# Four-head attention on one core: weighing rounds in two runs of three, maxima one slot sooner, three small VectorE operations on GpSimd

## The chip, the cores and the metric

The kernel runs on one core of a Trainium2 chip. The metric is the device time of one execution in microseconds (us). The core has a matmul engine (TensorE, in the rows PE, its weight loads PEld), three engines for elementwise work (VectorE or DVE, ScalarE or ACT, GpSimd or POOL) and SyncE, which issues transfers. Each engine runs its own list of instructions in order; semaphores tie the lists together. Matmul results land in PSUM, which has eight banks of 512 columns.

## What is computed

Two layers over 2048 rows of width 128; each layer is `x + s * silu(g)`, with an attention `s` and a feed-forward block `g`. The change lies in the attention inside `g` of the second layer: four heads of 32 columns, every row against all 2048 rows, with keys and values shared by the heads.

```
nx = _rmsnorm(X, g1)
Q = (nx @ Wq.T).reshape(B, S, H, dk).transpose(0, 2, 1, 3)
Kc = nx @ Wkc.T
Vc = nx @ Wvc.T
scores = jnp.einsum('bhsd,btd->bhst', Q, Kc) * scale
attn = jax.nn.softmax(scores, axis=-1)
out = jnp.einsum('bhst,btd->bhsd', attn, Vc)
out = out.transpose(0, 2, 1, 3).reshape(B, S, d) @ Wo.T
```

After it come a residual, a second norm, a router over eight experts and the experts themselves.

## The kernel before, in words

The 2048 query rows are cut into 16 tiles of 128. `shared_tile` of each engine is its work for one tile i; `over_tiles` calls it for 0 to 15. A tile has 16 slots t, one for each chunk of 128 keys.

In each slot TensorE makes one score matmul (L2050: keys of chunk t against the queries of all four heads, 512 columns) for tile i, and one maximum matmul (L2040: one head's queries against 512 keys) for a tile to come. ScalarE turns each score bank into exponentials in SBUF (L1543), VectorE reduces each maximum bank to one column (L1092). Scores rotate over three banks (2, 3, 4), maxima over three others (0, 1, 5): each engine can be at most three banks behind TensorE. A tile needs 16 maxima (`MU`); the first comes at slot `MAX_START` two tiles ahead, the last before the same slot one tile ahead.

The exponent needs the negated row maximum. Matmuls here take numbers rounded to a shorter format (fp32r), so the maximum, like the queries, is split into a high part and a low part, the rest. `cut_maximum` on VectorE makes the total (L1099), the high part (L1101) and the low part (L1103). `turn_maxima` (slot `TURN_SLOT` = 11) then transposes queries and maximum on TensorE (L2026, 98 rows), and ScalarE copies them (L1531); tile i+1's scores need that copy. Before, `turn_queries` (slot 6, L2017, 96 rows) transposed the queries of tile i+2 for the maxima, and ScalarE copied them (L1527) ahead of the exponentials of slot 6 and on. The queries' low part is a subtraction of VectorE in `query_tile` (L1131).

Weighing is the product of exponentials and values. Its 16 chunks are cut into six `ROUNDS`, five of three chunks and one of one. Three matmuls of a round work side by side on 32 columns each (L2060), and a fourth beside them (L2067) adds up the denominators. Its input is a sum of exponentials over chunks, made in `PIECES`: piece 0 is chunks 0 and 1, piece 1 is 2 to 4, piece 2 is 5 to 7, piece 3 is 8 to 10, piece 4 is 11 to 13. GpSimd makes these in `whole_sum`: a first addition (L773) and, for three chunks, a second (L778). The last piece (14, 15) is VectorE's (`last_sum`, L1109). The sums rotate over three buffers (`SUM_RING`): piece p waits for the round three before it. `ROUND_SLOT` says at the end of which slot a round stands in TensorE's list; 19 is slot 3 of the next tile. Before, this makes three runs of two rounds per tile: at slot 8, at slot 14 and at slot 3 of the next.

After the last round ScalarE copies the result (L1551), TensorE transposes it at slot 14 (`turn_rows`, L2074), VectorE takes the reciprocal of the denominators and adds the three parts (`shared_out`, L1119 and L1120), and a tile later divides (`shared_divided`, L1125). `PREP` puts preparations of the next stage into the list, one for each tile from 1 on: four projections or transposes at slot 2 or slot 9.

What follows is the code of this stage as far as the change reaches.

Of the kernel before, what the change touches and what calls it, by code (L numbers as in the profile page):

```python
# [6 lines left out]
P = 128  # L7
T = 2048
NT = T // P
D = 128  # L10
F32 = mybir.dt.float32
F32R = mybir.dt.float32r
# [3 lines left out]
ALU = mybir.AluOpType  # L16
# [25 lines left out]
HM = 4  # L42
DM = D // HM
SCM = float(DM) ** -0.5
R_ROWS = 3 * DM
# [6 lines left out]
NR = len(ROUNDS)  # L52
POOL_PIECES = NR - 1
SUM_RING = 3
ROUND_SLOT = (8, 8, 14, 14, 19, 19)
MU = HM * T // 512
MAX_BANKS = (0, 1, 5)
SCORE_BANKS = (2, 3, 4)
# [7 lines left out]
LAST_PREP = {(0, 2): ("omT", 3), (0, 4): ("mo", 3), (1, 1): ("nxT", 3), (1, 3): ("lg", 3)}  # L66
MAX_START = 9
QUERY_SLOT = 6
TURN_SLOT = 11
ROWS_SLOT = 14  # L70
OUT_SLOT = 14
SPLIT_SLOT = 3
OSTEPS = 2
SUM_PAIR = 2

E1 = 8
# [50 lines left out]
def at(a, i):  # L127

    if isinstance(i, int):
        return a[:, i]  # L130
    one = a[:, bass.ds(i, 1)]
    names = " ".join("abcd"[:len(one.shape) - 2])
    return one.rearrange(f"p o {names} -> p (o {names.split()[0]}) {' '.join(names.split()[1:])}")
# [8 lines left out]
def still(i, ahead):  # L142

    return not isinstance(i, int) or i + ahead < NT
# [34 lines left out]
def bass_recurrent_two_layers(nc, A, out):  # L179
# [4 lines left out]
    with ExitStack() as ctx:  # L184
# [117 lines left out]
        qkv = region.take(NT, D + 2 * DM)  # L302
        ka = region.take(NT, M_ROWS)
        crossT = region.take(T)
        qtile2 = region.take(2, HM, M_ROWS)
# [3 lines left out]
        om = region.take(NT, D)  # L309
        sp = region.take(SUM_RING, HM * P)  # L310
        mxp = region.take(HM, MU // HM)
        negm = region.take(HM)
        oT = region.take(HM * P)
        ol = region.take(HM, DM)
        rsm = region.take(HM)
# [75 lines left out]
        om_read = sem("om_read"); om_ready = sem("om_ready"); m_step = sem("m_step")  # L391
# [164 lines left out]
        def _(pool):  # L556
# [208 lines left out]
            def whole_sum(i, p, first):  # L765

                tiles = PIECES[p]
                o = sp[:, p % SUM_RING, :]
                held = lambda t: pm[:, t // 2 % HELD, t % 2 * HM * P:(t % 2 + 1) * HM * P]
                if not (first and p < SUM_RING):  # L770
                    pool.wait_ge(round_done, i * NR + p - SUM_RING + 1)
                pool.wait_ge(p_whole, i * NT + tiles[1] + 1)
                ins = pool.tensor_tensor(o, held(tiles[0]), held(tiles[1]), ALU.add)  # L773
                if len(tiles) == 3:
                    ins.then_inc(sum_step, 1)
                    pool.wait_ge(sum_step, i * (POOL_PIECES - 1) + p)
                    pool.wait_ge(p_whole, i * NT + tiles[2] + 1)
                    ins = pool.tensor_tensor(o, o, held(tiles[2]), ALU.add)  # L778
                ins.then_inc(sum_ready, 1)
# [3 lines left out]
            def low_rows(g):  # L783
                pool.wait_ge(xh_ready, g + 1)
                pool.tensor_tensor(xl[g], xnT[:, tokens(g)], xh[g].bitcast(F32), ALU.subtract).then_inc(xl_ready, 1)

            def shared_tile(i, parity, first=False, more=True):
                for p in range(POOL_PIECES):
                    whole_sum(i, p, first)
                if 0 <= i - HALVES_TILE < ES:  # L790
                    expert_halves(i - HALVES_TILE)
                if i in (6, 10, 14):
                    inverse_root(4, (i - 6) // 4, 1e-6)
                if i == 7:
                    low_rows(0)
# [35 lines left out]
        def _(dve):  # L831
# [251 lines left out]
                dve.wait_ge(rden_ready, (i + 1) // 2)  # L1083
                dve.tensor_tensor(o1T[:, (i - 1) * P:(i + 1) * P], parts[:, 0, :], rden[:, :], ALU.mult).then_inc(n_ready, 1)

            MSTEPS = 3

            def maximum(i, u):

                dve.wait_ge(mx_filled, i * MU + u + 1)  # L1090
                b = FIRST_BANKS[u % 5] if i == 0 else MAX_BANKS[(i * MU + u) % 3]
                dve.tensor_reduce(mxp[:, u // HM, u % HM:u % HM + 1], bank(b), AX.X, ALU.max).then_inc(mx_read, 1)  # L1092

            def cut_maximum(i, parity):

                high, low = (qtile2[:, parity, :, R_ROWS + n] for n in range(2))
                dve.wait_ge(mx_read, i * MU + MU)
                dve.wait_ge(tile_ready, i + 1)
                dve.tensor_reduce(negm[:, :], mxp[:, :, :], AX.X, ALU.max, negate=True).then_inc(m_step, 1)  # L1099
                dve.wait_ge(m_step, i * MSTEPS + 1)  # L1100
                dve.tensor_copy(high.bitcast(F32R), negm[:, :]).then_inc(m_step, 1)  # L1101
                dve.wait_ge(m_step, i * MSTEPS + 2)
                dve.tensor_tensor(low.bitcast(F32R), negm[:, :], high, ALU.subtract).then_inc(m_step, 1)  # L1103

            def last_sum(i):

# [15 lines left out]
            def shared_divided(i):  # L1122
                dve.wait_ge(om_read, OSTEPS * i + 2)
                dst = at(om, i).rearrange("p (h d) -> p h d", h=HM)
                dve.tensor_tensor(dst, ol[:, :, :], rsm[:, :].unsqueeze(2).broadcast_to([P, HM, DM]), ALU.mult).then_inc(om_ready, 1)  # L1125

            def query_tile(i, parity):

                q = at(qkv, i)[:, 0:D].rearrange("p (h d) -> p h d", h=HM)
                dve.wait_ge(q_high_ready, i + 1)  # L1130
                dve.tensor_tensor(qtile2[:, parity, :, 2 * DM:3 * DM].bitcast(F32R), q, qtile2[:, parity, :, 0:DM],  # L1131
                                  ALU.subtract).then_inc(q_low_ready, 1)
# [4 lines left out]
            for stage, i in chunk_order[:-1]:  # L1137
                if stage in steps:
                    steps[stage](i)
            cut_maximum(0, 0)  # L1140
            chunk_out(NT - 1)

            def residual1(g):
# [62 lines left out]
            def shared_tile(i, parity, first=False, more=True):  # L1206
                for t in range(NT):
                    for n, u in maxima_at(i, t):
                        if still(n, 0):
                            maximum(n, u)  # L1210
                            if u == MU - 1:
                                cut_maximum(n, 1 - parity)
                    if t == SPLIT_SLOT and still(i, 2):
                        query_tile(i + 2, parity)
                    if t == SPLIT_SLOT and i >= 2:
                        shared_divided(i - 2)
                    if t == 1 and not first:
                        last_sum(i - 1)
                    if t == 3 and i in (8, 12):
                        logits1((i - 8) // 4)  # L1220
                    if t == 4 and i in (6, 10, 14):
                        residual1((i - 6) // 4)
                    if t == 9 and i in (6, 10, 14):
                        row_stats((i - 6) // 4)
                        row_spread((i - 6) // 4)
                    if t == 9 and i == NT - 2:
                        router_differences(early_rows)
                    if t == 9 and i == NT - 1:
                        shares(early_rows, rexp_ready, 1)
                        largest(oh1, first_w, early_rows)  # L1230
                        first_place(oh1, early_rows)
                        without_first(early_rows)
                    if t == 10 and i == NT - 1:
                        logits1(2)
                        largest(oh2, second_w, early_rows)
                        first_place(oh2, early_rows)
                    if t == 12 and i == NT - 1:
                        weight_difference(early_rows)
                        router_differences(each_group[2])
                    if t == OUT_SLOT and not first:  # L1240
                        shared_out(i - 1)
# [1003 lines left out]
```

## Time and profile before

| What | Value |
|---|---|
| Median of three runs | 645.61 us (644.17 to 647.99) |
| Span of the profiled execution | 642.5 us |
| TensorE busy in it | 594.6 us, 93% |
| VectorE busy | 485.3 us, 76% |
| ScalarE busy | 351.0 us, 55% |
| GpSimd busy | 358.2 us, 56% |
| Stage of the change | 286.2 to 548.7 us |

The profile is of one execution; its span runs from the first instruction to the last, and the median of the runs is 3.1 us above it. Busy time is the sum over an engine's instructions. A wait is put down to the engine whose semaphore came last. Matmuls overlap with their successors, so the distance between two starts tells more than one duration.

### The profile page before, as it was taken

The numbers are of one execution on the slowest core, as the hardware profiler recorded it, in microseconds if no ns is written. First come the engines' busy times: TensorE is split into PE (matmuls) and PEld (weight loads), VectorE is DVE, ScalarE is ACT, GpSimd is POOL, SyncE is SP. The second block draws the span as 40 slices with busy tenths as digits, with TensorE's granted clock in tenths as the row PEclk, the third lists the DMA queues.
The fourth block names the chain that finished last, engine by engine and source line by source line (L and its number), as shares of the span: only waits on it lengthen the run. The fifth ranks groups of instructions, "written<-read, shape, count | busy, mean of one in ns | idle before, by whom it ended". The sixth has DMA issues, their size and how long they took to land.

```text
span 642.5 us, 12628 instructions
## 1 busy us (share of the span) xinstructions
PE 594.6 (93%) x4528; PEld 400.6 (62%) x4529; DVE 485.3 (76%) x1140; ACT 351.0 (55%) x710; POOL 358.2 (56%) x377
## 2 busy tenths in 40 slices
PE   4888899899989899969999999999999999999996
PEld 2566799667755566545555554555455543788885
DVE  5767345349968778898777787878887875798986
ACT  2645555336855456625777775767576665442222
POOL 6607400176647443607777778887787778415220
PEclk9999999999999999989999999999999998999998
DMA  9801122120000000000000000000000000000101
GB/s 294 347 2 50 51 66 65 41 55 6 0 2 2 2 3 3 3 1 1 1 1 1 1 2 1 2 0 2 1 2 1 1 2 1 1 2 1 34 0 34
DMA packets 16616, 17.33 MB, mean 27 GB/s; under 512 B 1712, under 2 KB 15024, under 8 KB 16176
## 3 DMA queue, kind: packets, MB, share of 16 engines
q1 hardware_dynamic: 15536, 14.49, 6.7%
q0 software_dynamic: 1024, 2.10, 1.1%
q8 instruction: 35, 0.57, 0.4%
q14 instruction: 21, 0.17, 0.1%
HBM read 11.34 MB, written 5.24 MB: 26 GB/s over the span
## 4 chain that ended last, share of the span: by engine, by line
PE 73%; DVE 12%; POOL 6%; issue 3%; ACT 3%; DMA 2%; SPq 0%; DVEq 0%; ACTq 0%; POOLq 0%
PE ps L2060 13%; PE ps L2050 10%; PE ps L2040 8%; PE ps L2188 5%; PE ps L1863 3%; DVE region L1092 3%; PE ps L1770 3%; PE ps L1753 3%; PE ps L2178 2%; PE ps L2180 2%; PE ps L2179 2%; POOL slots_in L626 2%; PE ps L1853 2%; PE ps L1951 2%; PE ps L1967 1%
## 5 line engine op out<-in xcount | busy, mean ns | idle before, releaser
L1092 DVE TENSOR_REDUCE region<-ps 128x1 f32<-128x512 f32 x256 | 160.7, 682 | 38.6 <-PE ps L2040 38.1
L1543 ACT ACTIVATE region<-ps 128x512 f32<-128x512 f32 x256 | 138.2, 600 | 58.7 <-PE ps L2050 58.7
L773 POOL TENSOR_TENSOR region<-region 128x512 f32<-128x512 f32 x80 | 108.9, 1364 | 42.2 <-ACT region L1543 38.5
L2050 PE MATMUL ps<-qmr,kr 98*128 98x512 f32 x256 | 111.9, 441 | 1.8 <-ACT region L1543 1.0
L2040 PE MATMUL ps<-kr,qmr 96*128 96x512 f32 x256 | 102.7, 411 | 2.2 <-DVE region L1092 1.5
L2060 PE MATMUL ps<-region 128*32 128x512 f32 x512 | 93.3, 609 | 0.0
L2067 PE MATMUL ps<-region,ones 128*32 128x512 f32 x192 | 93.1, 607 | 0.2 <-DVE region L1109 0.2
L778 POOL TENSOR_TENSOR region<-region 128x512 f32<-128x512 f32 x64 | 82.0, 1281 | 12.3 <-ACT region L1543 8.6
L2050 PEld LDWEIGHTS ps<-qmr,kr 98*128 98x128 f32 x256 | 48.8, 192 | 54.0 <-issue 28.8
L2040 PEld LDWEIGHTS ps<-kr,qmr 96*128 96x128 f32 x256 | 49.2, 193 | 15.5 <-DVE region L1092 9.0
L1647 ACT ACTIVATE region<-ps 128x512 f32<-128x512 f32 x36 | 21.6, 599 | 56.8 <-PE ps L2180 56.8
L664 POOL DMA_INDIRECT region<-slots_out,slot x16 | 15.2, 948 | 54.3 <-DMA slots_out<-og 49.7
L2060 PEld LDWEIGHTS ps<-region 128*32 128x32 f32 x512 | 18.8, 109 | 41.2 <-issue 27.7
L1265 DVE SCALAR_TENSOR_TENSOR xn<-ps,region,xn 128x128 f32<-128x128 f32 x144 | 40.5, 344 | 5.2 <-PE ps L2188 3.0
L1770 PE MATMUL ps<-region 128*128 128x128 f32 x272 | 37.0, 281 | 6.0 <-ACT region L1390 6.0
L1770 PEld LDWEIGHTS ps<-region 128*128 128x128 f32 x272 | 33.1, 191 | 11.7 <-ACT region L1390 11.2
L2188 PEld LDWEIGHTS ps<-e,region 128*128 128x128 f32 x288 | 36.9, 191 | 4.7 <-DVE region L1254 2.3
L2188 PE MATMUL ps<-e,region 128*128 128x128 f32 x288 | 38.5, 277 | 1.2 <-DVE region L1254 1.1
L1753 PE MATMUL ps<-region 128*128 128x512 f32 (+3 forms) x80 | 33.6, 554 | 3.9 <-ACT region L1378 2.5
L1390 ACT ACTIVATE region<-ps 128x512 f32<-128x512 f32 (+3 forms) x40 | 20.0, 531 | 22.8 <-PE ps L1762 22.5
L1378 ACT ACTIVATE region<-ps,nmax 128x1024 f32<-128x1024 f32 (+7 forms) x24 | 20.7, 865 | 19.6 <-DVE nmax L937 13.9
L933 DVE TENSOR_REDUCE rmax<-ps 128x1 f32<-128x512 f32 (+3 forms) x36 | 22.2, 623 | 11.5 <-PE ps L1753 11.0
(283 smaller groups left out, 1196.6 us busy)
## 6 DMA issues: line engine op xcount, KB each, us to landing
region<-in_w SPq DMA_DIRECT2D x2, 2048.0 KB, 12.8
slots_in<-zeros SPq DMA_DIRECT2D x1, 1536.0 KB, 9.0
region<-slots_in SPq DMA_DIRECT2D x6, 256.0 KB, 2.8
slots_out<-og SPq DMA_DIRECT2D x6, 256.0 KB, 2.4
e<-in_e SPq DMA_DIRECT2D x1, 1152.0 KB, 15.4
x<-in_x SPq DMA_DIRECT2D x4, 256.0 KB, 3.6
out<-y SPq DMA_DIRECT2D x3, 256.0 KB, 2.3
e<-in_e SPq DMA_DIRECT2D x1, 576.0 KB, 17.5
```

The source lines that it names most:

```text
L773: ins = pool.tensor_tensor(o, held(tiles[0]), held(tiles[1]), ALU.add)
L778: ins = pool.tensor_tensor(o, o, held(tiles[2]), ALU.add)
L1092: dve.tensor_reduce(mxp[:, u // HM, u % HM:u % HM + 1], bank(b), AX.X, ALU.max).then_inc(mx_read, 1)
L1265: dve.scalar_tensor_tensor(out=a_, in0=bank(4 + n_ % 2)[:, t * P:(t + 1) * P], scalar=c_, in1=a_, op0=ALU.mult, op1=ALU.add).then_inc(e_re ...
L1543: act.activation(pm[:, t // 2, t % 2 * HM * P:(t % 2 + 1) * HM * P], bank(SCORE_BANKS[n % 3]), ACT.Exp, scale=SCM).then_inc(p_whole, 1)
L1753: pe.matmul(scores_of(i)[:, c:c + m], qT[:, P * i:P * (i + 1)], kT[:, c:c + m], start=True, stop=True).then_inc(score_done, 1)
L1770: ins = pe.matmul(o[:, 0:D], probT[:, k % 2, P * (j - b):P * (j - b + 1)], v[:, j, :], start=(j == 0), stop=(j == i))
L2040: pe.matmul(bank(FIRST_BANKS[u % 5] if first else MAX_BANKS[(i * MU + u) % 3]), qm[0:R_ROWS, parity, h * P:(h + 1) * P], kr[0:R_ROWS, c:c ...
L2050: pe.matmul(bank(SCORE_BANKS[n % 3]), kr[0:M_ROWS, t * P:(t + 1) * P], qr[0:M_ROWS, parity, :], start=True, stop=True).then_inc(st_filled, 1)
L2060: pe.matmul(bank(6)[DM * g:DM * (g + 1), :], qkv[:, t, D + DM:D + 2 * DM], pm[:, t // 2 % HELD, t % 2 * HM * P:(t % 2 + 1) * HM * P], star ...
L2067: pe.matmul(bank(6)[DM * PARTS:P, :], ones[:, 0:DM], sp[:, r % SUM_RING, :], start=(r == 0), stop=(r == NR - 1), skip_group_check=True).th ...
L2188: ins = pe.matmul(bank(4 + n_ % 2)[:, t * P:(t + 1) * P], h1T[:, n_ % 2, t * P:(t + 1) * P], e2[:, e, :], start=True, stop=True)
```

## The change

`ROUND_SLOT` and `MAX_START` change, so weighing stands in two runs of three rounds (at slot 11 and at slot 3 of the next tile), and each maximum comes one slot sooner. The query subtraction, the division and the low part of the maximum go to GpSimd's list: the first two at the start of a tile, ahead of piece 0, the low part after piece 2. The very first low part, before tile 0, stays on VectorE, as do the last two divisions.

```diff
-ROUND_SLOT = (8, 8, 14, 14, 19, 19)
+ROUND_SLOT = (11, 11, 11, 19, 19, 19)
...
-MAX_START = 9
+MAX_START = 8
...
+MSTEPS = 3
+LOW_PIECE = 2
...
+            def query_low(i, parity):
+
+                q = at(qkv, i)[:, 0:D].rearrange("p (h d) -> p h d", h=HM)
+                pool.wait_ge(q_high_ready, i + 1)
+                pool.tensor_tensor(qtile2[:, parity, :, 2 * DM:3 * DM].bitcast(F32R), q, qtile2[:, parity, :, 0:DM],
+                                   ALU.subtract).then_inc(q_low_ready, 1)
+
+            def shared_divided(i):
+                pool.wait_ge(om_read, OSTEPS * i + 2)
+                dst = at(om, i).rearrange("p (h d) -> p h d", h=HM)
+                pool.tensor_tensor(dst, ol[:, :, :], rsm[:, :].unsqueeze(2).broadcast_to([P, HM, DM]), ALU.mult).then_inc(om_ready, 1)
+
+            def low_maximum(i, parity):
+
+                high, low = (qtile2[:, parity, :, R_ROWS + n] for n in range(2))
+                pool.wait_ge(m_step, i * MSTEPS + 2)
+                pool.tensor_tensor(low.bitcast(F32R), negm[:, :], high, ALU.subtract).then_inc(m_step, 1)
+
             def shared_tile(i, parity, first=False, more=True):
+                if still(i, 2):
+                    query_low(i + 2, parity)
+                if i >= 2:
+                    shared_divided(i - 2)
                 for p in range(POOL_PIECES):
                     whole_sum(i, p, first)
+                    if p == LOW_PIECE and more:
+                        low_maximum(i + 1, 1 - parity)
...
-            def cut_maximum(i, parity):
-
-                high, low = (qtile2[:, parity, :, R_ROWS + n] for n in range(2))
+            def high_maximum(i, parity):
+
                 dve.wait_ge(mx_read, i * MU + MU)
                 dve.wait_ge(tile_ready, i + 1)
+                if i > 0:
+                    dve.wait_ge(m_step, i * MSTEPS)
                 dve.tensor_reduce(negm[:, :], mxp[:, :, :], AX.X, ALU.max, negate=True).then_inc(m_step, 1)
                 dve.wait_ge(m_step, i * MSTEPS + 1)
-                dve.tensor_copy(high.bitcast(F32R), negm[:, :]).then_inc(m_step, 1)
-                dve.wait_ge(m_step, i * MSTEPS + 2)
-                dve.tensor_tensor(low.bitcast(F32R), negm[:, :], high, ALU.subtract).then_inc(m_step, 1)
+                dve.tensor_copy(qtile2[:, parity, :, R_ROWS].bitcast(F32R), negm[:, :]).then_inc(m_step, 1)
...
-                    if t == SPLIT_SLOT and still(i, 2):
-                        query_tile(i + 2, parity)
-                    if t == SPLIT_SLOT and i >= 2:
-                        shared_divided(i - 2)
```

What TensorE has in a row ahead of the turn of the maxima (L2026), in the kernel before; this is an ordinary tile, from the weighing at slot 8 on. L2060 and L2067 weigh, L2050 is a score, L2040 a maximum.

```order
L2060 MATMUL ps<-region 32x512 [waits p_whole] x3
L2067 MATMUL ps<-region,ones 32x512 [waits sum_ready]
L2050 MATMUL ps<-qmr,kr 128x512 [waits p_whole]
L2040 MATMUL ps<-kr,qmr 128x512 [waits mx_read,qm_ready]
L2050 MATMUL ps<-qmr,kr 128x512 [waits p_whole]
L2040 MATMUL ps<-kr,qmr 128x512 [waits mx_read]
L2050 MATMUL ps<-qmr,kr 128x512 [waits p_whole]
L2040 MATMUL ps<-kr,qmr 128x512 [waits mx_read]
L2026 MATMUL ps<-ident,region 98x128 [waits qm_ready,m_step]
```

The same place in the changed kernel: the last pair of the run, the turn (now L2047) and the weighing (L2081, L2088) behind it.

```order
L2071 MATMUL ps<-qmr,kr 128x512 [waits p_whole]
L2061 MATMUL ps<-kr,qmr 128x512 [waits mx_read]
L2047 MATMUL ps<-ident,region 98x128 [waits qm_ready,m_step]
L2047 MATMUL ps<-ident,region 98x128 x3
L2081 MATMUL ps<-region 32x512 [waits p_whole,oT_ready]
L2081 MATMUL ps<-region 32x512 [waits p_whole] x2
L2088 MATMUL ps<-region,ones 32x512 [waits sum_ready]
```

The weighing that stood three pairs ahead of the turn now stands behind it, and has a third round.

GpSimd's list over one tile before: one addition for piece 0, then pairs of additions for pieces 1 to 4, then one expert's subtraction.

```order
L773 TENSOR_TENSOR region<-region 128x512 [waits p_whole,round_done] x2
L778 TENSOR_TENSOR region<-region 128x512 [waits p_whole,sum_step]
L773 TENSOR_TENSOR region<-region 128x512 [waits p_whole,round_done]
L778 TENSOR_TENSOR region<-region 128x512 [waits p_whole,sum_step]
L726 TENSOR_TENSOR ehl<-e13,ehl 128x256 [waits eh_ready]
```

And in the changed kernel, where additions are L775 and L780: from the second addition of piece 1 on, to the first work of the next tile.

```order
L780 TENSOR_TENSOR region<-region 128x512 [waits p_whole,sum_step]
L775 TENSOR_TENSOR region<-region 128x512 [waits p_whole,round_done]
L780 TENSOR_TENSOR region<-region 128x512 [waits p_whole,sum_step]
L805 TENSOR_TENSOR region<-region 128x4 [waits m_step]
L775 TENSOR_TENSOR region<-region 128x512 [waits p_whole,round_done]
L780 TENSOR_TENSOR region<-region 128x512 [waits p_whole,sum_step]
L775 TENSOR_TENSOR region<-region 128x512 [waits p_whole,round_done]
L780 TENSOR_TENSOR region<-region 128x512 [waits p_whole,sum_step]
L728 TENSOR_TENSOR ehl<-e13,ehl 128x256 [waits eh_ready]
L793 TENSOR_TENSOR region<-region 128x4x32 [waits q_high_ready]
L799 TENSOR_TENSOR region<-region 128x128 [waits om_read]
```

L805 is the low part of the maximum, which `m_step` of the turn waits for; L793 is the query subtraction, L799 the division.

## Rows read from the trace of the kernel before

**Rows 1.** Chain that ended last: start us, length us, engine, line.

```profile
317.84 0.56 PE ps L2060 x3
...
333.71 0.56 PE ps L2060 x3
...
381.18 0.56 PE ps L2060 x3
...
398.63 0.56 PE ps L2060 x3
```

**Rows 2.** Busy time of each engine (instructions), clock, DMA in the stage.

```profile
286.20:548.70 262.50, 257.79 (x1480) 141.19 (x1480) 210.96 (x415) 175.13 (x363) 206.44 (x169) 0.98 0.00 1
```

**Rows 3.** Timeline of TensorE, tile 3: start us, length us, then the instruction.

```profile
338.94 0.63 PE L2060 MATMUL ps<-region 128*32 128x512 f32 x3
...
340.79 0.50 PE L2050 MATMUL ps<-qmr,kr 98*128 98x512 f32 x1
...
341.36 0.40 PE L2050 MATMUL ps<-qmr,kr 98*128 98x512 f32 x1
...
341.83 0.40 PE L2050 MATMUL ps<-qmr,kr 98*128 98x512 f32 x1
...
342.31 0.60 PE L2017 MATMUL ps<-ident,region 128*96 128x128 f32 x4
...
343.76 0.63 PE L2060 MATMUL ps<-region 128*32 128x512 f32 x3
...
345.62 0.50 PE L2050 MATMUL ps<-qmr,kr 98*128 98x512 f32 x1
...
347.13 0.60 PE L2026 MATMUL ps<-ident,region 128*98 128x128 f32 x4
...
348.98 0.60 PE L2074 MATMUL ps<-ident,region 128*128 128x128 f32 x4
```

**Rows 4.** Timeline of ScalarE, tile 3.

```profile
342.95 0.59 ACT L1527 ACTIVATE qmr<-ps 96x512 fp32r<-96x512 f32 x1 [0.47 <-PE ps L2017]
343.44 1.55 ACT L1543 ACTIVATE region<-ps 128x512 f32<-128x512 f32 x3
```

**Rows 5.** Timeline of GpSimd, tile 3; in brackets its idle time and releaser.

```profile
340.12 1.38 POOL L773 TENSOR_TENSOR region<-region 128x512 f32<-128x512 f32 x1 [0.21 <-PE ps L2067]
...
344.17 1.28 POOL L773 TENSOR_TENSOR region<-region 128x512 f32<-128x512 f32 x1 [0.75 <-ACT region L1543]
345.52 1.30 POOL L778 TENSOR_TENSOR region<-region 128x512 f32<-128x512 f32 x1
```

**Rows 6.** Timeline of VectorE, tile 3.

```profile
339.88 0.28 DVE L1131 TENSOR_TENSOR region<-region 128x128 fp32r<-128x128 f32 x1
...
341.56 3.14 DVE L1092 TENSOR_REDUCE region<-ps 128x1 f32<-128x512 f32 x5 [1.20 <-PE ps L2040]
344.73 0.17 DVE L1099 TENSOR_REDUCE region<-region 128x4 f32<-128x16 f32 x1
344.94 0.54 DVE L1101 CAST region<-region 128x4 fp32r<-128x4 f32 x1
...
350.13 0.53 DVE L1120 TENSOR_REDUCE region<-ps 128x128 f32<-128x384 f32 x1
```

**Rows 7.** Groups of GpSimd's instructions by form: count, busy us, mean ns.

```profile
L713 POOL TENSOR_TENSOR region<-region 128x128 fp32r<-128x128 f32 x4 | 1.8, 439 | 0.0
...
L598 POOL TENSOR_TENSOR msq<-msq,mv 128x4 f32<-128x4 f32 x4 | 0.8, 202 | 0.3
```

**Rows 8.** Tile 15: two stretches as in rows 2, then TensorE's timeline.

```profile
532.30:534.30 2.00, 1.53 (x5) 0.56 (x3) 1.34 (x2) 2.00 (x7) 1.69 (x2) 1.00 0.01 4
...
536.60:539.90 3.30, 3.30 (x17) 0.63 (x10) 0.00 (x0) 1.27 (x3) 2.67 (x3) 0.50 0.00 0
...
536.97 1.09 PE L2060 MATMUL ps<-region 128*32 128x512 f32 x3
...
537.82 1.09 PE L2060 MATMUL ps<-region 128*32 128x512 f32 x3
```

More of the change, by code:

```diff
@@ L1084, in chunk_out @@
                 dve.tensor_tensor(o1T[:, (i - 1) * P:(i + 1) * P], parts[:, 0, :], rden[:, :], ALU.mult).then_inc(n_ready, 1)
-            MSTEPS = 3
             def maximum(i, u):
@@ L1139, in _ @@
                     steps[stage](i)
-            cut_maximum(0, 0)
+            high_maximum(0, 0)
+            dve.wait_ge(m_step, 2)
+            dve.tensor_tensor(qtile2[:, 0, :, R_ROWS + 1].bitcast(F32R), negm[:, :], qtile2[:, 0, :, R_ROWS], ALU.subtract).then_inc(m_step, 1)
             chunk_out(NT - 1)
@@ L1211, in shared_tile @@
                             if u == MU - 1:
-                                cut_maximum(n, 1 - parity)
-                    if t == SPLIT_SLOT and still(i, 2):
-                        query_tile(i + 2, parity)
-                    if t == SPLIT_SLOT and i >= 2:
-                        shared_divided(i - 2)
+                                high_maximum(n, 1 - parity)
                     if t == 1 and not first:
```

## The prediction

> **What bounds the kernel now.** I read the busy time by stage first. In the stage that the change touches, 286.2 to 548.7 us, TensorE is busy 257.8 of 262.5 us; VectorE, ScalarE and GpSimd stand idle for 52, 87 and 56 us of it [rows 2]. The chain of waits shows the same weighing matmul returning every 15.87 us in an ordinary tile (317.84 to 333.71) and every 17.45 us in tiles 6 and 10 (381.18 to 398.63), where the rows of a finished group are also added and measured [rows 1]. So TensorE's row of instructions sets the time. Whatever is taken off another engine is worth nothing by itself; what counts is what TensorE does and how long it stands.
>
> TensorE works in order. Tile 3 gives its clockwork [rows 3]. Call T the end of the weighing at slot 3, where the score of slot 4 starts (340.79). From T to the next weighing (343.76) come five pairs of score and maximum and four query transposes: 2.97 us. A pair inside a run takes 0.47 us (341.36 to 341.83); the first one after weighing takes 0.57 (340.79 to 341.36). A weighing of two rounds takes 1.85 us (338.94 to 340.79) or 1.86 (343.76 to 345.62), and a round is two steps of 0.43, since two neighbouring steps stand 0.85 apart at half clock [rows 8]. The turn of the maxima comes at 347.13, which is T + 6.34.
>
> **What it gives.** One entry into and exit from weighing per tile goes: 1.86 less 4 x 0.43 is 0.13, the slower first pair is 0.10, and I add as much for the slower entry: 0.3 us per tile, 15 tiles, 5 us. This part is sure and on TensorE itself.
>
> The subtraction of the queries (0.28 us), the division (the same size) and the low part of the maximum leave VectorE [rows 6]. They ran beside a weighing, when VectorE had emptied its banks (it waits for TensorE before 341.56 and again after the cut), so TensorE never waited for them: worth 0 in time. If that cover were absent, it would be about 0.7 us a tile.
>
> **What it costs: the turn of the maxima.** It needs the low part of the negated maximum. That part is now GpSimd's, and stands behind both additions of piece 2 (chunks 5, 6, 7). When are those done? Follow the chain from T: TensorE turns the queries at 342.31, T + 1.52 [rows 3]; ScalarE copies them at 342.95 and only then takes the exponentials of slots 6, 7 and 8 from 343.44 on [rows 4]; GpSimd adds chunks 5 and 6 at 344.17, 0.13 after exponential 6 ends, and chunk 7 at 345.52 [rows 5]. None of this moves relative to T: the query turn stays at slot 6, and GpSimd comes free earlier than it needs to, since piece 0 can begin once round 3 is done (before, piece 1 began at 340.12 after the first round of that weighing; now piece 0 begins 1.5 us before T, and its three additions of 1.35 us and the wait for exponential 4 end at T + 2.7, before T + 3.38). The next instruction of GpSimd can start 1.35 after 345.52, at T + 6.08. A 128x4 operation of GpSimd takes 0.20 us [rows 7], with 0.1 for the signal: the low part is there at T + 6.4.
>
> Before, that instant was harmless, because TensorE had 1.86 us of weighing between slots 8 and 9 and reached the turn at T + 6.34 anyway. Now the weighing stands behind the turn. TensorE reaches it after 2.97 + 3 x 0.47 - 0.09 = T + 4.3. It waits **2.1 us**. Queued behind it on TensorE are all three rounds, then slots 12 to 15; ScalarE and GpSimd wait for those. In tiles 5, 7, 9, 11 and 13 four transposes of outputs or rows at slot 9 stand ahead of it (0.44 us by 347.13 to 348.98 less three pairs), and the wait is 1.65. Other waits fall inside this one and cost nothing more: exponential 6 is late for the score of slot 9 by 0.4, and the maximum of slot 11 has to wait for VectorE to T + 4.8.
>
> Bounds of the unknown op: GpSimd's low part costs between 0 beyond its additions (wait 1.8) and the 0.44 us of its own 128x128 subtraction (wait 2.4); 0.20 is the same shape, so I take that.
>
> **What it costs: longer runs without weighing.** VectorE reads a bank in 0.61 us, (3.14 - 0.68) / 4 [rows 6], TensorE fills one in 0.47, and three banks are in turn. Runs of five and six pairs were short enough; runs of eight are not. In slots 12 to 19 VectorE starts 0.77 after the first score (341.56 against 340.79), reads three banks, spends 0.6 on the reciprocal and sum of the output (0.53 for the sum), and has read slot 15 at 3.9; TensorE wants to fill the bank of slot 18 at 3.6. Cost 0.3 us, between 0 and 0.6. In slots 4 to 11 the lag hides in the 2.1.
>
> **Other moves.** The query subtraction and division on GpSimd (about 0.44 each by the 128x128 subtraction there [rows 7]) end some 2 us before piece 0 may start: 0. Maxima one slot sooner need the copied queries at T + 2.75 where TensorE asks at T + 2.65: inside the wait.
>
> **Sum.** An ordinary tile: +2.1 + 0.3 - 0.3 = +2.1, six tiles (1 to 4, 8, 12): 12.6. Tiles 5, 7, 9, 11, 13: +1.65, 8.3. Tiles 6 and 10 already have 1.6 us of stalls, and the query turn that starts the chain is late in them already; +1.2 each, 2.4, between 0.5 and 2.1. Tile 0 (bound by VectorE) and tile 14 (no new maxima, but the same wait): 1.8 each, 3.6. Tile 15 has no turn; its last weighing is a round longer and one entry goes: 0, up to 2 either way. Together +27 us on a span of 642.5, so 669.5. The median is 3.1 above that span: **672.6 us**.
>
> **The skill against the row.** Rows: on shapes alike VectorE subtracts 128x128 in 0.28 us [rows 6], GpSimd in 0.44 [rows 7]. The Trainium skill, GPSIMD Engine Reference, section 4.1, says to keep two-input elementwise work on VectorE, since GpSimd is about twice as slow; the rows give 1.5 times. By either figure the operation's own length is a few tenths; it is its place in the row that costs, and the sum stays.
>
> **Rivals.** (a) The clock falls. At 536.6 the granted clock dropped to 0.50 for 3.3 us (that is 1.2 of 2.4 GHz) after a stretch in which TensorE was busy 1.53 of 2.00 us (its first half) [rows 8]. The stretch from T + 2.7 to T + 6.4 will be emptier than that one. Each fall costs half of 3.3, some 1.7 us, and mostly hits weighing. In five tiles: 8 us, 681; in all fourteen 24, 696. Against: such falls come only sometimes in that spot, and tiles 6 and 10 stalled with the stage's mean clock at 0.98 [rows 2]. The Trainium skill, TensorE: Matmul & The Clock Gate, section on HAM oscillation, ties the fall to TensorE standing idle for long; no wait as long as the coming 2 us is in this stage, and the row at 536.6 fell after shorter ones, so I do not rely on it. (b) The low part is not what holds: if GpSimd reaches it before T + 4.9, only VectorE's lag remains, 0.6 to 0.8 per tile with the other run, less 0.3: 15 x 0.5, 653. Against: row 345.52. (c) Faster: both waits vanish and only the saved entries stay, -5: 641. It decides at one point, whether the turn can start by T + 4.4, for which the low part would have to be done 1.7 us before the additions ahead of it; for it speaks only that VectorE sheds 0.7 us a tile. (d) The change does nothing that shows: the gain of 5 and VectorE's lag cancel, 645.6.
>
> **How the numbers follow.** Forecast 0.65 (663 to 679); clock 0.20 (679 to 698); lag only 0.06; faster 0.05; nothing 0.04. The range runs from 657 (a wait of 1.2 instead of 2.1 in thirteen tiles) to 690 (2.4, and the clock falls in seven tiles). A measurement here can tell some 0.5%, 3 us, from no change. Faster 0.05, same 0.04, slower 0.91.
>
> **What would show it.** In the trace after: transposes of the maxima (98 rows) preceded by an idle TensorE of 1 to 2 us, released by GpSimd's 128x4 subtraction; that subtraction right behind a 1.28 us addition, 6.1 us after T; ordinary tiles 18 us apart and odd ones 17.4; weighing in two runs of 2.7 us; a short wait for VectorE near slot 18. I am wrong if the turn starts by T + 5, if the tiles stay at 15.9, or if GpSimd has finished chunk 7 before T + 5.

## The result

The changed kernel takes 677.49 us (676.06 to 678.41) against 644.89 us for the kernel before: 1.0491 times as long, 95% interval 1.0458 to 1.0524. The forecast was slower, 672.6 us, in a range of 657 to 690. The profiled execution has a span of 675.5 us, 33.0 more than before. Of these, 31.1 lie in the stage of the change, from the first turn of the maxima to the last weighing step: 262.8 us before (284.3 to 547.1), 293.9 after (286.6 to 580.5). Ahead of the stage 2.3 us were added, 1.7 of them by one more fall of TensorE's clock (at 275.5), and behind it 0.4 fell away.

Busy time of the stage in the kernel after, columns as in [rows 2]. TensorE is now busy 273.9 of 292.5 us, where it was 257.8 of 262.5, and its mean clock is 0.96 instead of 0.98.

```profile
288.40:580.90 292.50, 273.90 (x1479) 141.22 (x1480) 195.78 (x369) 174.70 (x363) 215.28 (x212) 0.96 0.00 1
```

TensorE's waits over the whole execution after: who waited for what, us in total, times, longest. The first row is the turn of the maxima waiting for GpSimd's low part, the second a maximum waiting for VectorE. Neither line had 2 us in this stage before.

```profile
PE ps L2047 <- POOL region L805: 8.1, 15, 1.9
...
PE ps L2061 <- DVE region L1116: 5.7, 13, 0.6
```

TensorE in tile 4, the same part of a tile as [rows 3]. T is again the start of the score of slot 4, behind the weighing of slot 3: here 367.96, and 374.19 is the turn of the maxima, T + 6.23. Before it stand two idle times: 0.57 us ahead of the maximum of slot 11 (373.30, T + 5.34), for VectorE, and 0.39 us ahead of the turn, for GpSimd. The weighing that follows runs at half clock: its two steps are 0.85 apart, not 0.43.

```profile
367.96 0.50 PE L2071 MATMUL ps<-qmr,kr 98*128 98x512 f32 x1
...
373.30 0.50 PE L2061 MATMUL ps<-kr,qmr 96*128 96x512 f32 x1 [0.57 <-DVE region L1116]
374.19 0.84 PE L2047 MATMUL ps<-ident,region 128*98 128x128 f32 x4 [0.39 <-POOL region L805]
374.96 1.07 PE L2081 MATMUL ps<-region 128*32 128x512 f32 x3
...
375.81 1.07 PE L2081 MATMUL ps<-region 128*32 128x512 f32 x3
```

GpSimd and VectorE at the same place. GpSimd's two additions of piece 2 and then the low part stand close to where [rows 5] put them, at T + 3.38, T + 4.75 and T + 5.97. VectorE's cast of the high part (L1126) took 1.14 us where it had taken 0.54 [rows 6]. Both casts end within 0.05 us of the end of GpSimd's first addition (371.34 + 1.29 here; 344.17 + 1.28 before).

```profile
371.34 1.29 POOL L775 TENSOR_TENSOR region<-region 128x512 f32<-128x512 f32 x1 [0.76 <-ACT region L1564]
372.71 1.27 POOL L780 TENSOR_TENSOR region<-region 128x512 f32<-128x512 f32 x1
373.93 0.20 POOL L805 TENSOR_TENSOR region<-region 128x4 fp32r<-128x4 f32 x1
```

```profile
371.52 1.14 DVE L1126 CAST region<-region 128x4 fp32r<-128x4 f32 x1
```

TensorE's granted clock fell four times in the stage after tile 0, for 3.4, 3.4, 3.4 and 6.8 us. Three falls come as the turn of the maxima starts, in tiles 2, 4 and 12, and lie on the weighing behind it; the fourth is tile 15's and twice as long as the one of [rows 8]. Here are stretches inside three of them, columns as in [rows 2]; the one of tile 12 (517.9) looks like that of tile 4.

```profile
375.00:377.80 2.80, 2.80 (x17) 0.75 (x20) 0.04 (x1) 0.60 (x1) 0.79 (x1) 0.50 0.00 0
...
337.10:340.20 3.10, 3.10 (x15) 0.81 (x18) 0.53 (x1) 0.60 (x1) 0.48 (x1) 0.50 0.02 5
...
569.20:575.70 6.50, 6.50 (x30) 2.00 (x29) 1.68 (x10) 1.24 (x3) 3.67 (x3) 0.50 0.00 1
```

Tile 3 has the same two waits and no fall: its weighing, at 356.89, runs at full clock.

```profile
355.43 0.50 PE L2061 MATMUL ps<-kr,qmr 96*128 96x512 f32 x1 [0.58 <-DVE region L1116]
356.32 0.65 PE L2047 MATMUL ps<-ident,region 128*98 128x128 f32 x4 [0.39 <-POOL region L805]
```

### The profile page after: what moved, and what is told of

Same layout as the page of the kernel before. It is cut to its first block, busy times and chain, and to the rows that moved or that the text cites. A ratio compares the mean times of both kernels' runs of the same rounds, so it can differ in the third digit from the quotient of the medians.

```text
span 675.5 us, 12628 instructions
## 1 busy us (share of the span) xinstructions
PE 613.7 (91%) x4528; PEld 402.8 (60%) x4529; DVE 470.7 (70%) x1097; ACT 350.5 (52%) x710; POOL 368.9 (55%) x420
## 4 chain that ended last, share of the span: by engine, by line
PE 56%; DVE 15%; POOL 12%; ACT 8%; issue 6%; DMA 2%; SPq 0%; POOLq 0%; DVEq 0%; ACTq 0%
PE ps L2081 13%; DVE region L1116 7%; ACT region L1564 5%; POOL region L780 5%; PE ps L2209 5%; PE ps L1884 3%; PE ps L1791 3%; PE ps L2061 3%; PE ps L2199 2%; PE ps L1774 2%; PE ps L2201 2%; PE ps L2200 2%; POOL slots_in L628 2%; PE ps L1874 2%; PE ps L2071 2%
## 5 line engine op out<-in xcount | busy, mean ns | idle before, releaser
L1564 ACT ACTIVATE region<-ps 128x512 f32<-128x512 f32 x256 | 135.8, 603 | 59.1 <-PE ps L2071 55.2
L775 POOL TENSOR_TENSOR region<-region 128x512 f32<-128x512 f32 x80 | 101.7, 1279 | 67.3 <-PE ps L2088 46.5
L2061 PE MATMUL ps<-kr,qmr 96*128 96x512 f32 x256 | 106.9, 428 | 7.2 <-DVE region L1116 5.7
L2088 PE MATMUL ps<-region,ones 128*32 128x512 f32 x192 | 95.2, 634 | 0.4 <-POOL region L780 0.4
L2081 PE MATMUL ps<-region 128*32 128x512 f32 x512 | 95.5, 640 | 0.0
L780 POOL TENSOR_TENSOR region<-region 128x512 f32<-128x512 f32 x64 | 81.6, 1276 | 8.6 <-ACT region L1564 4.6
L2081 PEld LDWEIGHTS ps<-region 128*32 128x32 f32 x512 | 21.2, 116 | 51.5 <-issue 47.0
L1668 ACT ACTIVATE region<-ps 128x512 f32<-128x512 f32 x36 | 21.6, 599 | 56.8 <-PE ps L2201 56.8
L1791 PEld LDWEIGHTS ps<-region 128*128 128x128 f32 x272 | 33.1, 191 | 11.7 <-ACT region L1411 11.2
L1774 PE MATMUL ps<-region 128*128 128x512 f32 (+3 forms) x80 | 32.0, 533 | 3.9 <-ACT region L1399 2.5
L1275 DVE TENSOR_TENSOR region<-region,ps 128x512 f32<-128x512 f32 x36 | 24.7, 685 | 7.4 <-ACT region L1668 4.2
## 6 DMA issues: line engine op xcount, KB each, us to landing
e<-in_e SPq DMA_DIRECT2D x1, 1152.0 KB, 15.7
```

The costliest lines, as they stand in the source:

```text
L1564: act.activation(pm[:, t // 2, t % 2 * HM * P:(t % 2 + 1) * HM * P], bank(SCORE_BANKS[n % 3]), ACT.Exp, scale=SCM).then_inc(p_whole, 1)
L1774: pe.matmul(scores_of(i)[:, c:c + m], qT[:, P * i:P * (i + 1)], kT[:, c:c + m], start=True, stop=True).then_inc(score_done, 1)
L1791: ins = pe.matmul(o[:, 0:D], probT[:, k % 2, P * (j - b):P * (j - b + 1)], v[:, j, :], start=(j == 0), stop=(j == i))
L2061: pe.matmul(bank(FIRST_BANKS[u % 5] if first else MAX_BANKS[(i * MU + u) % 3]), qm[0:R_ROWS, parity, h * P:(h + 1) * P], kr[0:R_ROWS, c:c ...
L2081: pe.matmul(bank(6)[DM * g:DM * (g + 1), :], qkv[:, t, D + DM:D + 2 * DM], pm[:, t // 2 % HELD, t % 2 * HM * P:(t % 2 + 1) * HM * P], star ...
L2088: pe.matmul(bank(6)[DM * PARTS:P, :], ones[:, 0:DM], sp[:, r % SUM_RING, :], start=(r == 0), stop=(r == NR - 1), skip_group_check=True).th ...
```

## The experiments

The theory that the result suggests: TensorE is held by two waits in parallel, and the later one counts. One is GpSimd's low part, ready for T + 6.2. The other is VectorE, whose cast cannot run beside GpSimd's addition, so that it reads the bank of slot 8 too late for the maximum of slot 11, T + 5.3. Experiments 1 to 4 ran on a chip where the kernel before took 645.65 us, 5 to 12 on one where it took 666.8. The difference between the chips lies ahead of the stage; the stage itself has the same length on both (260.3 us for the same kernel in experiments 3 and 11, 293.9 and 293.8 for the changed kernel). So ratios to the kernel before on the same chip are given, and lengths of the stage. The last column is the time that TensorE's granted clock was at half in the stage, tile 0 left out; while TensorE is busy, half of that time is lost. Stage and clock are of one profiled execution each, and the falls differ from one execution to the next: in experiment 1 the mean clock of the whole kernel was 0.986 in the profiled execution and 0.974 to 0.983 in the others.

| Run | Ratio to before (95%) | Stage, us | Weighing of slot 11 starts | Half clock, us |
|---|---|---|---|---|
| kernel before | 1 | 262.8 | (slots 8, 14) | 3.4 |
| changed kernel | 1.0491 (1.0458 to 1.0524) | 293.9 | T + 6.8 | 17.1 |
| 1 low part on VectorE | 1.0334 (1.0292 to 1.0377) | 281.5 | T + 6.4 | 3.4 |
| 2 turn behind weighing | 1.0208 (1.0173 to 1.0243) | 275.3 | T + 5.76 | 3.4 |
| 3 moves only | 0.9959 (0.9937 to 0.9982) | 260.3 | (slots 8, 14) | 0 |
| 4 as 1, high part by reduction | 1.0271 (1.0226 to 1.0316) | 281.1 | T + 6.2 | 10.2 |
| 5 high part by reduction | 1.0421 (1.0384 to 1.0459) | 292.8 | T + 6.8 | 17.1 |
| 6 as 2 and 5 | 1.0054 (1.0031 to 1.0078) | 267.8 | T + 4.94 | 6.8 |
| 7 tables only | 1.0313 (1.0272 to 1.0354) | 281.8 | T + 6.4 | 3.4 |
| 8 as 2, maxima from slot 9 | 1.0068 (1.0045 to 1.0091) | 267.6 | T + 4.93 | 6.8 |
| 9 as 6 and 8, queries at slot 4 | 1.0162 (1.0115 to 1.0210) | 275.3 | T + 4.95 | 17.1 |
| 10 as 3, high part by reduction | 0.9986 (0.9955 to 1.0017) | 260.9 | (slots 8, 14) | 0 |
| 11 moves only, again | 0.9961 (0.9937 to 0.9985) | 260.3 | (slots 8, 14) | 0 |
| 12 changed kernel, again | 1.0430 (1.0388 to 1.0472) | 293.8 | T + 6.8 | 17.1 |

**1. The low part back on VectorE.**

```diff
-                    if p == LOW_PIECE and more:
-                        low_maximum(i + 1, 1 - parity)
...
+                    dve.wait_ge(m_step, i * MSTEPS + 2)
+                    dve.tensor_tensor(qtile2[:, parity, :, R_ROWS + 1].bitcast(F32R), negm[:, :], qtile2[:, parity, :, R_ROWS], ALU.subtract).then_inc(m_step, 1)
```

> The changed kernel with one part undone: the low part of the maximum is again VectorE's, right behind the high part; GpSimd keeps the query subtraction and the division. T is the first score after the weighing at slot 3. In the changed kernel the turn of the maxima starts at T + 6.23. Theory A (the place of the low part behind GpSimd's additions holds the turn, as the prediction has it): the turn goes at T + 4.9 to 5.1, 1.2 us sooner in 14 tiles, 677.5 - 17 = about 660. Theory B (VectorE's own lag holds nearly as long: its cast of the high part ends only with GpSimd's addition at T + 4.70, the bank for the maximum of slot 11 is read at T + 5.3): the turn goes at T + 5.7, 0.5 us sooner, about 670. Theory C (the split into two runs costs by the clock, not by waits): no change, 677.

It took 667.43 us. In tile 4 (T = 364.20) the turn starts at T + 5.86: GpSimd's wait is gone and VectorE's has grown to 0.79. Theory A falls, B holds. TensorE, then VectorE:

```profile
369.73 0.50 PE L2062 MATMUL ps<-kr,qmr 96*128 96x512 f32 x1 [0.79 <-DVE region L1114]
370.06 0.60 PE L2048 MATMUL ps<-ident,region 128*98 128x128 f32 x4
```

```profile
367.74 1.14 DVE L1124 CAST region<-region 128x4 fp32r<-128x4 f32 x1
368.91 0.17 DVE L1127 TENSOR_TENSOR region<-region 128x4 fp32r<-128x4 f32 x1
```

The stage is 12.4 us shorter than in the changed kernel, more than the 0.4 us that a tile gains (turns 17.47 apart instead of 17.87, in 13 tiles 5.2). Most of the rest is the clock: no tile before the last has a fall here, and tile 15 has a short one, 3.4 us at half clock instead of 17.1, which is worth 6.8.

**2. The turn behind the weighing.**

```diff
-                    if t == TURN_SLOT and more:
-                        turn_maxima(i + 1, 1 - parity)
...
                     for r in rounds_at(t):
                         weigh(i, r, first)
+                    if t == TURN_SLOT and more:
+                        turn_maxima(i + 1, 1 - parity)
```

> The changed kernel with TensorE's turn of the maxima put behind the weighing of slot 11 instead of ahead of it; nothing else moves. GpSimd's low part then has 2.7 us of weighing as cover. Theory A: the weighing starts at T + 4.4 to 5 instead of T + 6.8, 677.5 - 27 = about 650. Theory B: the maximum of slot 11 still waits for VectorE until T + 5.3, the weighing starts at T + 5.65, 1.15 us sooner, of which the turn's 0.53 is paid behind it: 0.6 x 14 = 8.5, about 669.

659.57 us. The weighing starts at T + 5.76, where B had T + 5.65. The time is 9 us below B's: 6.8 of them are the clock, since this run too has no fall before tile 15, and tile 14, whose turn had waited 1.9 us for the low part, gains 2.1 us (its turns 15.07 apart instead of 17.20) where B counted 0.6. The maximum of slot 11 still waits for VectorE:

```profile
367.71 0.51 PE L2061 MATMUL ps<-kr,qmr 96*128 96x512 f32 x1 [0.58 <-DVE region L1116]
368.14 0.63 PE L2081 MATMUL ps<-region 128*32 128x512 f32 x3
```

**3. The moves alone.**

```diff
-ROUND_SLOT = (11, 11, 11, 19, 19, 19)
+ROUND_SLOT = (8, 8, 14, 14, 19, 19)
-MAX_START = 8
+MAX_START = 9
```

> The changed kernel with the two tables set back (weighing at slots 8, 14 and 19, maxima from slot 9): only the three moves from VectorE to GpSimd are left. Theories A and B: GpSimd has the low part at T + 6.2, the turn comes at T + 6.34 behind the weighing of slot 8 anyway, so the moves are worth nothing, 643 to 646. Theory D (the moves themselves cost, through additions that GpSimd starts later or slows): 650 or more.

643.24 us, ratio 0.9959. The moves cost nothing, and the low part is no hindrance in this order, though by little: in tile 3 GpSimd has it done at 348.86 and TensorE comes to the turn at 349.01, because the weighing of slot 8 stands ahead of it. D falls. The small gain comes back under 11.

**4. The high part by reduction, low part on VectorE** (on top of experiment 1).

```diff
-                dve.wait_ge(m_step, i * MSTEPS + 1)
-                dve.tensor_copy(qtile2[:, parity, :, R_ROWS].bitcast(F32R), negm[:, :]).then_inc(m_step, 1)
+                dve.tensor_reduce(qtile2[:, parity, :, R_ROWS].bitcast(F32R), mxp[:, :, :], AX.X, ALU.max, negate=True).then_inc(m_step, 1)
```

> The first experiment, and the high part of the maximum is now made by a second reduction of the 16 partial maxima straight into the rounded format instead of a cast of the total, so that it need not wait for GpSimd's addition. Theory A (only the low part's place counted): as the first experiment, no further gain. Theory B (the cast blocked by GpSimd is the larger part of the wait): VectorE goes on reading at T + 3.9 instead of T + 4.6, the turn starts at T + 4.9 to 5.0, 1.3 us sooner than in the changed kernel in 14 tiles: 677.5 - 18 = about 659, 10 below the first experiment.

664.13 us, and the turn, at T + 5.66, only 0.2 sooner. Neither A nor B as written. VectorE's rows show why: the reduction takes 0.16 us beside GpSimd's addition (365.74 to 367.03), but now the subtraction, with two inputs in SBUF, is the one that is held until that addition ends.

```profile
365.80 0.16 DVE L1123 TENSOR_REDUCE region<-region 128x4 fp32r<-128x16 f32 x1
366.00 1.05 DVE L1126 TENSOR_TENSOR region<-region 128x4 fp32r<-128x4 f32 x1
```

This execution has 6.8 us more at half clock than that of experiment 1; without the clock its stage would be 3.8 us shorter, not 0.4.

**5. The high part by reduction in the changed kernel**, low part on GpSimd; the same edit, with a wait for the reduction before the next maximum.

> The changed kernel with the high part of the maximum made by a reduction instead of a cast, so that VectorE need not wait for GpSimd's addition; the low part stays on GpSimd, the turn ahead of the weighing. Theory E (two waits in parallel, the later one counts: VectorE's lag lets the maximum of slot 11 start at T + 5.3, GpSimd's low part lets the turn start at T + 6.2): the first goes, the second stays, the turn starts at T + 6.2 as before, 674 to 678. Theory B alone (VectorE's blocked cast is the cause and the low part only comes along): the turn starts at T + 5, about 660.

The ratio is 1.0421; the time of 695.65 us is that of the other chip. Theory E is met: VectorE's wait is gone, the maximum of slot 11 starts at T + 4.60 (392.87, T = 388.27), and all of the waiting is now GpSimd's, 1.22 us at once.

```profile
392.87 0.40 PE L2061 MATMUL ps<-kr,qmr 96*128 96x512 f32 x1
394.50 0.64 PE L2047 MATMUL ps<-ident,region 128*98 128x128 f32 x4 [1.22 <-POOL region L805]
```

Against the same kernel without the edit on this chip (12, 1.0430) the two cannot be told apart.

**6. Both holds taken away**: the edits of 2 and 5.

> Both holds taken away: high part by reduction and the turn behind the weighing of slot 11, low part on GpSimd. Theory E: VectorE reads on at T + 3.9 instead of T + 4.6, the weighing starts at T + 5.0 instead of T + 5.76 in the second experiment, 14 x 0.7 = 10 below its 659.6, about 650. Theory F (VectorE's 0.61 us per bank against TensorE's 0.47 in a run of eight pairs is what remains, whatever the cast does): 656 or more.

Ratio 1.0054, in a stage of 267.8 us, 7.5 below experiment 2, and 9.3 below it with the clock taken out. Theory E foresaw 10 below it and T + 5.0; measured is T + 4.94 (368.32, T = 363.38). F falls. VectorE's second reduction no longer waits for anything:

```profile
366.83 0.16 DVE L1125 TENSOR_REDUCE region<-region 128x4 fp32r<-128x16 f32 x1
367.02 2.48 DVE L1116 TENSOR_REDUCE region<-ps 128x1 f32<-128x512 f32 x4
```

**7. The tables alone** in the kernel before.

```diff
-ROUND_SLOT = (8, 8, 14, 14, 19, 19)
+ROUND_SLOT = (11, 11, 11, 19, 19, 19)
-MAX_START = 9
+MAX_START = 8
```

> The kernel before with the two tables of the change alone (weighing at slots 11 and 19, maxima from slot 8); all three small operations stay on VectorE. Theory E: as the first experiment, 667, since the low part there was VectorE's too and the query subtraction and the division lie beside weighing: 664 to 670. Theory G (the moved subtraction and division relieve VectorE in the longer runs): 672 or more.

Ratio 1.0313, stage 281.8 us, against 1.0334 and 281.5 in experiment 1: the moved query subtraction and division are worth nothing either way, and G falls. So in the stage the tables cost 19 us by themselves, and the place of the low part another 12, of which 6.8 are the clock.

**8. Maxima from slot 9, turn behind weighing.**

```diff
-MAX_START = 8
+MAX_START = 9
```

> The second experiment (turn behind the weighing), with maxima from slot 9 as in the kernel before. The cut of the maximum then comes after VectorE has read the bank of slot 8, so the maximum of slot 11 does not wait for the blocked cast. Theory E: the weighing starts at T + 4.7 instead of T + 5.76, 14 x 1.0 below 659.6, about 646. Theory F (the lag of the long run itself): the maximum of slot 11 still waits, 656 or more.

Ratio 1.0068, stage 267.6 us. The cast is there, but it comes one read later, when GpSimd's addition is nearly over (0.55 us), and the maximum of slot 11 does not depend on what follows it. That is as good as experiment 6, and F falls. The size that E had foreseen was missed: T + 4.93 instead of T + 4.7, and a ratio of 1.0068 where E's 646 would be 1.0005. Taking the maxima a slot sooner is what put the cast in front of the bank that TensorE needs.

**9. Everything together, and the queries turned at slot 4.**

```diff
-QUERY_SLOT = 6
+QUERY_SLOT = 4
```

> The two-run order with everything taken away that held TensorE so far: high part by reduction, maxima from slot 9, turn of the maxima behind the weighing; and the turn of the queries at slot 4 instead of 6, so that exponential 6 no longer waits behind the copy of the queries. Theory H (what is left of the 0.65 us between T + 4.29 and T + 4.94 is the score of slot 9 waiting for exponential 6): the weighing starts at T + 4.55, 14 x 0.35 = 5 us below the eighth experiment, level with the kernel before. Theory F (VectorE's lag in a run of eight): no change against the eighth experiment, 0.6% above the kernel before.

Ratio 1.0162: worse, which neither theory foresaw, and H falls. In ordinary tiles the weighing starts at T + 4.95, as in experiment 8. The copy of the queries now delays exponential 4 instead of 6, and from there ScalarE takes 0.5 us per exponential and TensorE follows it. In tiles 6 and 10 the weighing starts at T + 8.1 and T + 8.6, where experiment 8 had T + 5.6. The turn of the queries now waits up to 1.5 us for the residual, with two slots less work ahead of it, and in both tiles the clock fell behind that wait. Of the 7.7 us by which the stage is longer than in experiment 8, 5.1 are the clock. In an ordinary tile (T = 378.4) ScalarE makes eight exponentials in 3.99 us without a gap, from 380.11 on, and TensorE's score of slot 7 waits 0.23 us for the first of them.

**10. The moves alone, high part by reduction.**

> The third experiment (the moves to GpSimd alone, tables as before) with the high part by reduction. TensorE hardly waits there, so a VectorE that is freed by 0.6 us a tile should give nothing in ordinary tiles and at most 0.3 us in tiles 6, 10 and 14: within 0.2% of the third experiment. If VectorE's blocked cast costs hidden time in the kernel before, it is 0.5% or more faster.

Ratio 0.9986 (0.9955 to 1.0017), the stage 0.6 us longer than in 3, which is no more than the longer fall in tile 0 costs here (8.0 us at half clock in that tile instead of 6.4). No gain, as expected; the distance to experiment 3 is 0.3% and not the 0.2% foreseen, within the intervals.

**11. The moves alone, five rounds.**

> The third experiment again, with more rounds: it was 0.4% faster than the kernel before, where nothing was expected. If the gain is real: 0.3 to 0.5% again. If not: within 0.1%.

0.9961 (0.9937 to 0.9985): the gain of 0.4% is there again. The stage is 2.5 us shorter than before. In the executions profiled, 1.7 us of it is a fall of the clock in tile 15 (536.6, [rows 8]) that neither of the two runs has. Why it stays away was not tried, and whether other executions have it is not known. This is the fastest version of the study, 0.4% ahead of the kernel before.

**12. The changed kernel again.**

> The changed kernel itself, to see how many falls of the clock its tiles take in another execution, and whether its ratio holds on this chip: 1.045 to 1.052, with two to four falls of TensorE's clock within the stage that the first experiment, with the same slots, does not have.

Ratio 1.0430, a little under the 1.045 to 1.052 foreseen. The stage is 293.8 us, again with three falls in tiles 2, 4 and 12 and a long one in tile 15.

## Why the prediction was right, and where it was off

**Direction, place and size.** Right. Ordinary tiles were to become 2.1 us longer: in tiles 2, 4 and 12 the turns of the maxima stand 17.87 to 17.90 apart instead of 15.87, 2.0 more. Odd tiles from 5 on were to become 1.65 longer: 17.11 instead of 15.7 in tile 9, 1.4 more. Tiles 6 and 7 take 36.09 us together instead of 33.27, 2.8 more for a forecast of 2.85; tiles 10 and 11 take 35.71 instead of 33.25, 2.5 more. GpSimd's low part starts at T + 5.97 for a forecast of T + 6.08, takes 0.20 us as taken from [rows 7], and the turn starts at T + 6.23 for T + 6.4. The weighing takes two runs of 2.7 us, and slot 18 has its short wait. (The distances in tiles 3, 5 and 13 have a fall of the clock in them and come below.)

**The total is nearer than its parts, and that is luck.** The span grew by 33.0 us for a forecast of 27. Without the clock the stage grew by 24.5, and this is made of errors that partly cancel: tiles 1 to 14 are 2.1 us shorter than the sum had them; tile 0, counted at 1.8 longer, became 0.7 shorter; tile 15, counted at 0, became 2.2 longer, for a reason that was not looked for. The falls of the clock then added 6.6 us in the stage, and 1.9 came from outside it. The bounds have a slip as well: a wait of 1.2 instead of 2.1 us in thirteen tiles takes 11.7 from 672.6 and gives 661, not the 657 at which the range begins. And 0.44 against 0.28 us is 1.6 times, not 1.5.

**The clock.** It was a rival with chance 0.20, and it came beside the forecast instead of in its place: three falls at 1.66, 1.63 and 1.64 us (turns 19.54 apart instead of 17.88, 18.73 and 18.74 instead of 17.10), and a fall in tile 15 that lasted 6.8 us instead of 3.4, some 1.7 more. The prediction expected an idle time of 2 us at once and still gave the falls only 0.20, since tiles 6 and 10 had stalled without one. What came was smaller, 0.57 and 0.39 us one behind the other, and the clock fell at 374.5. The Trainium skill, TensorE: Matmul & The Clock Gate, has a section on a second failure mode, where short idle times between groups of matmuls, in another kernel, make the clock swing; the prediction had weighed only the section on long idle times. The trace agrees with the second as far as falls after short idle times go; tile 3 shows that the same waits need not bring one.

**The step that was wrong in its reason.** The prediction gave the whole 2.1 us to the low part and had VectorE let the maximum of slot 11 go at T + 4.8, "inside" that wait. Measured is T + 5.34, and the pure wait for GpSimd is 0.39; the idle time of 1 to 2 us ahead of the turn that was to show the forecast did not appear. The mis-sized term is the cast: T + 4.8 comes out with the 0.54 us of [rows 6] as its length, but that is the time to the end of GpSimd's addition, and in the new order VectorE comes to it 0.6 us sooner (T + 3.56 instead of T + 4.15) and is held 0.6 us longer. The wait has two causes in parallel, so taking the low part away gives 0.4 us a tile (experiment 1), taking the cast away gives nothing (5), and taking both away gives 1.9 (6: the weighing at T + 4.94 instead of T + 6.8), less the turn's own 0.5, which then stands behind it. Rival (b) of the prediction, "only VectorE's lag", is what experiment 1 makes; it priced it at 653, and it is 667, since the held cast was not in the price. With both holds away (6), a tile is 0.5 us longer than before, as (b) had it.

**The gain.** The 0.3 us of the saved entry, of which 0.1 is an estimate, could not be isolated, and no run shows it by itself: experiments 6 and 8 still come out 0.5 us a tile longer than before, with 0.65 us lost ahead of slot 11 and some 0.25 at slot 18. The 0.65 has no single place, as 9 shows: in experiment 8 the score of slot 9 waits 0.24 us for exponential 6, and if that is mended, another exponential is late.

**The moves.** Forecast 0 for the query subtraction and the division, measured 0 in the two-run order (7 against 1). All three together make the old order 0.4% faster (3 and 11).

## What to carry to other kernels

Before work is moved behind or ahead of a waiting instruction of the busiest engine, ask what used to pass the time until its operand was ready; the weighing at slot 8 looked like an interruption and was the cover for a chain of copy, exponential and two additions. An operand on the busiest engine's path should not stand in another engine's list behind long operations that it does not need. And when two waits end close together, removing either shows little: take both away before judging.

## What the runs showed of the hardware

A VectorE instruction that casts 128x4 elements from SBUF to SBUF, or subtracts them with both inputs in SBUF, does not run beside a GpSimd addition of 128x512 that started before it: it ends 0.02 to 0.03 us behind that addition. Measured are 0.54, 0.55 and 1.14 us for the cast and 1.05 and 1.21 for the subtraction (1.21 in tile 9 of the kernel before, at 441.79, so its trace had the hold already), against 0.17 for either when it starts between two additions (the shortest of the 16 casts of the changed kernel, whose median is 1.14, and the subtraction at 368.91 in experiment 1). Reductions with one SBUF input took 0.16 to 0.17 in the midst of the same additions. It works the other way round too: in the kernel before, an addition of GpSimd that starts while VectorE's own addition of 128x512 is under way (L1109, 0.68 us, from 338.08) takes 1.74 to 1.76 us instead of 1.28, thirteen times in the stage.

```profile
338.15 1.75 POOL L773 TENSOR_TENSOR region<-region 128x512 f32<-128x512 f32 x1 [1.19 <-ACT region L1543]
```

The Trainium skill, SBUF — State Buffer, section "Who interferes with whom", says it: the two engines share a pair of ports, the one that starts first holds it for its whole instruction, and only VectorE instructions with two SBUF inputs or in a mode that uses both ports are concerned. The trace agrees on who waits and until when; in which mode the cast ran no row shows. A copy can be kept out by writing it as a reduction (experiments 5 and 6).

TensorE's clock fell from 2.4 to 1.2 GHz after short idle times. In the changed kernel it fell in tiles 2, 4 and 12, in each of two executions, behind waits of 0.57 or 0.58 and 0.38 to 0.40 us. Tiles 1, 3, 6, 8 and 10 have the same two waits and no fall, and tile 14, which waits 1.9 us at once, has none either. With one wait of 1.2 us at the turn (experiment 5) the clock fell in tiles 3 and 10, and behind one of 1.7 us in tile 14. In the orders without the wait for GpSimd it did not fall in tiles 1 to 13, except in tiles 6 and 10 of experiment 9. These counts suggest that the waits bring the falls; what decides in which tile they come was not found.
